# Projection, row mixing and a top-2 mixture of experts: one program section in place of two, with two expert tiles at fixed places between the last routing steps

## The chip, the cores and the metric

The program runs on one core of one Trainium2 chip. The metric is the device time of one execution in microseconds (us); less is better. Engines are named as in the profile: PE is TensorE's matrix multiply, PEld its weight load, DVE is VectorE, ACT is ScalarE, POOL is GpSimd, SP is SyncE. POOLq, SPq and so on are an engine's own queue, that is what it does beside computing: waiting, branching, issuing transfers.

## The reference, cut to what matters

```python
x = x + _L0_xattn_ref(_layernorm(x), ctx_4096, ctx_4096, Wq, Wk, Wv, Wo)   # 32 batches of 32 rows, 257 context rows, 32 heads, 8 key heads
x = x + _L0_attn_ref(_layernorm(x), eta)
x = x + _L0_ffn_ref(_layernorm(x), gate_w, expert_w)

def _L0_attn_ref(minibatch, eta):
    logits = jnp.einsum('bcl,bdl->bcd', minibatch, minibatch)
    probs = jax.nn.softmax(jnp.max(logits, axis=-1, keepdims=True) - logits, axis=-1)
    return eta * jnp.einsum('bcd,bdl->bcl', probs, minibatch) + minibatch

def _L0_ffn_ref(x, gate_w, expert_w):                     # 8 experts of 1024 x 1024, top 2
    topv, topi = jax.lax.top_k(jnp.einsum('bsh,he->bse', x, gate_w), 2)
    w_e = jnp.einsum('bske,bsk->bse', jax.nn.one_hot(topi, 8), jax.nn.softmax(topv, axis=-1))
    return jnp.einsum('bsh,eho,bse->bso', x, expert_w, w_e)
```

All is float32. x has 1024 rows (tokens) of 1024 values; each row goes to two of eight experts. With the reference's own inputs the experts get 244, 303, 297, 182, 250, 268, 260 and 244 rows; in tiles of 128 rows these are 2, 3, 3, 2, 2, 3, 3 and 2, together 20 tiles. Of the first 640 tokens, 148 go to expert 0 and 185 to expert 1.

## The kernel before, in words

The program has three sections, each a block that all engines enter and leave together: `attend` (L210), `mixing` (L874) and `experts` (L1302).

**attend** is the cross attention, up to the turned head outputs `oT`. The change touches one line of it (L525).

**mixing** works on eight tiles of 128 tokens (four batches of 32) in ten steps, t = 0 to 9, unrolled. In step t the engines handle three tiles at once, in an order written out by hand:
- PE (L1258) does the output projection of tile t in eight units of six matmuls (three passes of high and low parts, L1245), and between units the rest: before unit 2 the mixing product of tile t-2 (L1274, with the gate columns L1278), before unit 4 the transposes of the normalized rows y of tile t-1 (L1254), before unit 5 the ranking product of tile t-2 (L1266, L1267), before unit 6 the gate product (L1288, eight matmuls) and the gram product of 32 x 32 blocks (L1293) of tile t-1.
- DVE (L1103): add x to the projection and normalize it to y (L1111, L128, L132), scale and add the mixed rows (L1121), route (L1153: logits, the gap of the two best L1163, their one-hot rows), normalize to n (L132 again), low part of the next tile's oT (L1098), ranks and row numbers (L1170), the softmax shares of tile t-1 (L1135 to L1148).
- POOL (L1021): the power of -1/2 for both norms (L142), x3 = x2 + z (L1036), and two indirect DMAs per tile that put a token's number and weight into its expert's list `slot_scratch` (L1041).
- ACT (L1073): high parts, copies of transposes (L1071), exponentials, and from step 7 on the high parts of experts 0 and 1 (L1091; low parts on DVE, L871).
- SP (L981) loads x, stores n and x3 (which goes to `out_x`), and loads the raw weights of expert 0 at step 2 and of expert 1 at step 8.

After the last step PE counts the rows per expert (L1299), DVE works out a table `tiles` (L1197 to L1229: 30 small dependent instructions) that gives each tile's expert and number within the expert, and POOL gathers the rows of tile 0 (L1057).

**experts** runs 20 tiles in the order of the experts (L1474 for PE; tiles from number 8 on are behind a branch on the table). For each: gather 128 rows of n by the list into `xg` (L1369), transpose (L1469), split in high (L1408) and low (L1433), 48 matmuls of 128 x 512 (L1487), gather the rows of `out_x` into `acc` (L1387), multiply-add (L1458), and scatter them back to `out_x` (L1393). A token is in two experts, so POOL waits before each gather of `acc` for the scatter of the tile before it:

```python
            def step(i, par):                                   # POOL, L1379
                pool.wait_ge(gT_done, 2 * i + 2)
                gather(i + 2, par)
                wait_apart(pool, written, 16 * i, passed)
                ...
                pool.indirect_dma_start(acc[:, par, :], None, out, ...)
                ...
                wait_apart(pool, acc_ready, 2 * i + 2, passed)
                pool.indirect_dma_start(out, ..., acc[:, par, :], None, ...).then_inc(written, 16)
```

Weights of expert e+1 are split into the other of two slots while expert e runs: chunks 0 to 3 in its first tile's step, chunks 4 to 7 at the head of its second tile's step (L1445 to L1453 on DVE, L1418 on ACT). DVE's step i is, in this order: splits, low part of tile i+1 (L1433), splits, wait for `acc` of tile i and multiply-add.

Of the kernel before, what the change touches and what calls it, by code (L numbers as in the profile page):

```python
# [12 lines left out]
ALU = mybir.AluOpType  # L13
# [39 lines left out]
class Shared:  # L53


    def __init__(self, nc, ctx):
# [11 lines left out]
        self.tiles = sb("tiles", [1, 7, COLS], I32)  # L68

        self.first_raw = [self.at("expert0_raw", LOW0, [P, KC, D]), self.at("expert1_raw", LOW1, [P, KC, D])]  # L70
# [5 lines left out]
        self.w_h_ready, self.w_l_ready = sem("w_h_ready"), sem("w_l_ready")  # L76

        self.idx = sb("idx", [P, 2, 2], I32)
        self.xg = self.at("xg", STAGE, [P, 2, D])
        self.idx_loaded, self.xg_loaded = sem("idx_loaded"), sem("xg_loaded")  # L80


def pipelined(eng, n, step, head=1, tail=1):


    assert head % 2 == 1
    pairs = (n - head - tail) // 2
    for t in range(head):
        step(t, t % 2)
    with eng.Fori(0, pairs) as i:  # L90
        step(2 * i + head, head % 2)
        step(2 * i + head + 1, (head + 1) % 2)
    for t in range(head + 2 * pairs, n):
        step(t, t % 2)
# [12 lines left out]


class Norm:

    def __init__(self, nc, ctx, name):
        self.stats = ctx.enter_context(nc.sbuf_tensor(name + "_stats", [P, 2, 6], F32))
        self.mean_var = ctx.enter_context(nc.sbuf_tensor(name + "_mean_var", [P, 2], F32))
        self.rstd = ctx.enter_context(nc.sbuf_tensor(name + "_rstd", [P, 1], F32))
        self.var_eps = ctx.enter_context(nc.sbuf_tensor(name + "_var_eps", [P, 1], F32))
        self.minus_half = ctx.enter_context(nc.sbuf_tensor(name + "_minus_half", [P, 1], F32))
        self.eps_added = ctx.enter_context(nc.semaphore(name + "_eps_added"))
        self.passed = ctx.enter_context(nc.semaphore(name + "_passed"))  # L120
        self.stats_ready = ctx.enter_context(nc.semaphore(name + "_stats_ready"))
        self.var_ready = ctx.enter_context(nc.semaphore(name + "_var_ready"))
        self.rstd_ready = ctx.enter_context(nc.semaphore(name + "_rstd_ready"))

    def on_vector(self, dve, t, out, src):

        for h in range(2):
            dve.bn_stats(self.stats[:, h, :], src[:, h * 512:(h + 1) * 512]).then_inc(self.stats_ready, 1)  # L128
        wait_apart(dve, self.stats_ready, 2 * t + 2, self.passed)
        dve.bn_aggr(self.mean_var[:, :], self.stats[:, :, :].rearrange("p a b -> p (a b)")).then_inc(self.var_ready, 1)  # L130
        dve.wait_ge(self.rstd_ready, t + 1)
        return dve.tensor_scalar(out, src, self.mean_var[:, 0:1], self.rstd[:, 0:1], ALU.subtract, ALU.mult)  # L132

    def start_gpsimd(self, pool):
        pool.memset(self.minus_half[:, :], -0.5).then_inc(self.eps_added, 1)
        pool.wait_ge(self.eps_added, 1)

    def on_gpsimd(self, pool, t):
        wait_apart(pool, self.var_ready, t + 1, self.passed)
        pool.tensor_scalar(self.var_eps[:, :], self.mean_var[:, 1:2], EPS, None, ALU.add).then_inc(self.eps_added, 1)  # L140
        pool.wait_ge(self.eps_added, t + 2)
        pool.tensor_tensor(self.rstd[:, :], self.var_eps[:, :], self.minus_half[:, :], ALU.pow).then_inc(self.rstd_ready, 1)  # L142

class LayerNorm:

# [1385 lines left out]
```

## Time and profile before

| | us |
|---|---|
| median of 3 executions (1200.42 to 1202.53) | 1201.32 |
| the profiled execution | 1197.56 |
| its span, first to last instruction | 1195.3 |
| PE busy / DVE / ACT / POOL | 1078.9 / 683.6 / 441.2 / 265.7 |
| mean granted clock of PE, of full speed | 0.948 |

The span is what the trace shows; the profiled execution is 2.26 us longer than it. Busy shares over the whole span mix the attention section (to 717 us, not changed) with the two sections that are changed, so they say little here: the stages have to be read one by one.

### The profile page before, as it was taken

The page shows a single profiled execution, that of the slowest core. Times are in us where ns is not written, and L with a number is a line of the kernel's source. Part 1 is how long each engine was busy: PE and PEld are TensorE (multiplying, and loading weights), DVE is VectorE, ACT ScalarE, POOL GpSimd, SP SyncE. Part 2 cuts the span into 40 slices and gives each one's busy share as a digit, 9 for nine tenths or more (in the row PEclk, how much of TensorE's full clock was granted, in tenths as well). Part 3 has the DMA queues.
Part 4 walks back from the last instruction along what each step waited for, and adds up shares of the span by engine and source line. Part 5 has one row for each costly group of instructions (what it writes and reads, how often), then busy time and mean ns, then how long its engine had stood idle before and what let it go on. Part 6 is the DMA issues. An engine that isn't in the chain of part 4 may idle for free. (4 is left out here: it accounts for less than half of the span.)

```text
span 1195.3 us, 26103 instructions
## 1 busy us (share of the span) xinstructions
PE 1078.9 (90%) x9084; PEld 987.0 (83%) x9085; DVE 683.6 (57%) x1683; ACT 441.2 (37%) x1079; POOL 265.7 (22%) x454
## 2 busy tenths in 40 slices
PE   6899989999999999999999968999717988888995
PEld 5799989999999999999999947778616766766784
DVE  5541256666666666666666672787773334444441
ACT  2321245555555555555555461111240312333210
POOL 2000211111112112111111101443322333332342
PEclk9899999999999999999999968999857989999997
DMA  8233566656656755665675451653515546565422
GB/s 312 83 125 128 178 179 195 185 169 182 201 159 183 204 165 176 194 173 168 196 201 164 117 178 57 212 106 90 192 56 170 203 172 223 181 218 213 155 88 68
DMA packets 78810, 197.76 MB, mean 165 GB/s; under 512 B 14672, under 2 KB 25296, under 8 KB 74608
## 3 DMA queue, kind: packets, MB, share of 16 engines
q1 hardware_dynamic: 60688, 154.04, 41.3%
q0 software_dynamic: 18016, 42.29, 11.5%
q8 instruction: 68, 1.11, 0.4%
q14 instruction: 38, 0.31, 0.1%
HBM read 159.07 MB, written 44.56 MB: 170 GB/s over the span
## 5 line engine op out<-in xcount | busy, mean ns | idle before, releaser
L510 ACT ACTIVATE prob<-bank,nmax 128x257 f32<-128x257 f32 x256 | 122.0, 477 | 242.0 <-DVE nmax L650 241.7
L650 DVE TENSOR_REDUCE nmax<-bank 128x1 f32<-128x257 f32 x256 | 108.7, 425 | 157.2 <-PE bank L843 157.2
L1487 PE MATMUL bank<-w_h,gT_h 128*128 x320 | 132.0, 412 | 28.2 <-DVE gT_l L1433 28.2
L739 PE MATMUL bank<-wkv_h,cT_h 128*128 128x256 f32 x512 | 154.4, 302 | 0.0
L730 PE MATMUL bank<-cT_h,wkv_h 128*128 128x256 f32 x512 | 154.4, 302 | 0.0
L730 PE MATMUL bank<-cT_h,wkv_l 128*128 128x256 f32 x512 | 144.5, 282 | 0.0
L739 PE MATMUL bank<-wkv_h,cT_l 128*128 128x256 f32 x512 | 144.5, 282 | 0.0
L730 PE MATMUL bank<-cT_l,wkv_h 128*128 128x256 f32 x512 | 144.1, 282 | 0.0
L739 PE MATMUL bank<-wkv_l,cT_h 128*128 128x256 f32 x512 | 143.9, 281 | 0.0
L403 POOL DMA_DIRECT2D qcat<-q_scratch x128 | 70.4, 557 | 270.0 <-PE bank L843 267.0
L1487 PE MATMUL bank<-w_l,gT_h 128*128 x320 | 128.8, 402 | 0.0
L1487 PE MATMUL bank<-w_h,gT_l 128*128 x320 | 128.5, 401 | 0.0
L765 PE MATMUL bank<-ident,prob 128*128 128x128 f32 x512 | 101.4, 280 | 10.1 <-DVE pT L303 7.0
L1408 ACT ACTIVATE gT_h<-bank 128x512 fp32r<-128x512 f32 x42 | 22.9, 595 | 216.3 <-PE bank L1469 216.3
L1487 PEld LDWEIGHTS bank<-w_h,gT_h 128*128 128x128 f32 x320 | 62.8, 196 | 43.4 <-issue 30.9
L730 PEld LDWEIGHTS bank<-cT_l,wkv_h 128*128 128x128 f32 x512 | 97.4, 190 | 0.0
L642 DVE TENSOR_SCALAR prob<-prob,rsums 128x257 f32<-128x257 f32 x256 | 92.1, 360 | 9.1
L739 PEld LDWEIGHTS bank<-wkv_l,cT_h 128*128 128x128 f32 x512 | 97.3, 190 | 0.0
L730 PEld LDWEIGHTS bank<-cT_h,wkv_h 128*128 128x128 f32 x512 | 97.2, 190 | 0.1
L739 PEld LDWEIGHTS bank<-wkv_h,cT_h 128*128 128x128 f32 x512 | 97.2, 190 | 0.0
L730 PEld LDWEIGHTS bank<-cT_h,wkv_l 128*128 128x128 f32 x512 | 96.8, 189 | 0.0
L739 PEld LDWEIGHTS bank<-wkv_h,cT_l 128*128 128x128 f32 x512 | 96.6, 189 | 0.0
(203 smaller groups left out, 2440.6 us busy)
## 6 DMA issues: line engine op xcount, KB each, us to landing
kcat<-k_scratch SPq DMA_DIRECT2D x128, 258.0 KB, 4.2
cx<-in_context SPq DMA_DIRECT2D x32, 1024.0 KB, 7.3
raw<-in_expert_w SPq DMA_DIRECT2D x48, 512.0 KB, 6.3
qcat<-q_scratch POOLq DMA_DIRECT2D x128, 128.0 KB, 3.2
k_scratch<-kT_h SPq DMA_DIRECT2D x32, 258.0 KB, 2.8
k_scratch<-kT_l SPq DMA_DIRECT2D x32, 258.0 KB, 2.9
x_in<-in_x SPq DMA_DIRECT2D x16, 512.0 KB, 6.3
expert_raw<-in_expert_w SPq DMA_DIRECT2D x16, 512.0 KB, 8.8
```

Source lines behind the costliest of these rows:

```text
L403: pool.dma_start(qcat[c * DH:(c + 1) * DH, par, :, :].rearrange("d (g j) n -> d g (j n)", g=4).bitcast(F32), q_dram[c // 2, b].rearrange(" ...
L510: act.activation(prob[:, 1 - par, s, 0:SK], s_ps[s % 2][:, 0:SK], ACT.Exp, bias=nmax[:, 1 - par, s:s + 1], accum_out=sums[:, 1 - par, s:s ...
L642: dve.tensor_scalar(prob[:, a % 2, i, 0:SK], prob[:, a % 2, i, 0:SK], rsums[:, i:i + 1], None, ALU.mult).then_inc(prob_ready, 1)
L650: dve.reduce_max(nmax[:, 1 - par, s:s + 1], s_ps[s % 2][:, 0:SK], AXX, negate=True).then_inc(max_done, 1)
L730: o = pe.matmul(k_ps[:, j * 256:(j + 1) * 256], wkv[w][:, k, j * P:(j + 1) * P], cT[t][:, b % 2, k, :], start=(j == 0 and k == 0 and n == ...
L739: o = pe.matmul(v_ps[:, a * KV:(a + 1) * KV], cT[t][:, b % 2, k, a * P:(a + 1) * P], wkv[w][:, k, KV:2 * KV], start=(a == 0 and k == 0 and ...
L765: o = pe.transpose(turn_ps[:, c * P:(c + 1) * P], prob[:, a % 2, i, c * P:(c + 1) * P], ident[:, :])
L1408: act.activation(gT[0][:, par, h * 512:(h + 1) * 512], t_ps[h][:, :], ACT.Copy).then_inc(gT_h_ready, 1)
L1487: o = pe.matmul(y_ps[par][h][:, :], gT[a][:, par, k * P:(k + 1) * P], w[b][:, bass.ds(slot + (k * D + h * 512), 512)], start=(k == 0 and n ...
```

## The change

`mixing` and `experts` become one function `finish`, one block, with these edits:

1. **Gate columns in the gram product.** The 32 columns of each batch in `yT` get 8 gate columns beside them, so one product with 40 columns gives the gram block and the gate logits. The gate is loaded four times, once for each batch of a tile. L1288 goes.
2. **PE waits at the start.** PE waits for the constants and the small loads (gate, eta) before the projection of tile 0; before, it did so ahead of step 1.
3. **Norms.** n is made by ACT (scale and shift) in place of DVE; x3 is x2 + y on POOL, with the mixed rows added in place by DVE. The two one-hot instructions become one.
4. **Expert 0's weights early.** `oT` is laid out by tiles, its raw weights are loaded at the start, and one chunk is split in each step from 1 to 7.
5. **Two fixed tiles.** The first 128 rows of expert 0 and of expert 1 among the first five tiles of tokens are gathered in step 7 and multiplied between the last routing products. (Were there fewer than 128, the lists would be padded.)
6. **The plan** leaves these two tiles out, has 32 instructions in 11 dependent groups, and is followed by the other 18 tiles.
7. **POOL's step** gathers `acc` of tile i+1 after the scatter of tile i, and waits only for scatters of other experts' tiles, and for the buffer: `written` is one semaphore for each of the two buffers.

```diff
-        self.oT = self.at("oT", HIGH0, [P, KC, B * SQ])
+        self.oT = self.at("oT", HIGH0, [P, NT, KC, P])
...
+FIXED = 2
+EARLY = NT - 3
...
@@ SP @@
-            sp.dma_start(gate_sb[:, :, :], gate.rearrange("(c p) e -> p c e", p=P)).then_inc(small_loaded, 16)
+            for b in range(BT):
+                sp.dma_start(yT[:, :, b, SQ:GW], gate.rearrange("(c p) e -> p c e", p=P)).then_inc(small_loaded, 16)
...
+                if t == EARLY + 2:
+                    sp.wait_ge(scattered, 32 * EARLY)
+                    for i in range(FIXED):
+                        sp.dma_start(idx[:, i, :], fixed_rows(i)).then_inc(fixed_idx_loaded, 16)
+                        sp.dma_start(idx_out[:, i, :], fixed_rows(i)).then_inc(fixed_idx_loaded, 16)
...
@@ POOL @@
+            pool.wait_ge(scattered, 32 * NT)
+            pool.wait_ge(plan, PLANNED)
+            pool.wait_ge(xg_loaded, 16 * FIXED)
+            for i in range(2, 4):
+                load_idx(idx, i, i % 2).then_inc(idx_loaded, 16)
+            scatter(0, 0)
+            pool.wait_ge(gT_done, 2)
...
+            gather(2, 0)
+            pool.wait_ge(x2_ready, 2 * NT)
+            pool.wait_ge(written[0], 16)
+            gather_out(1, 1)
...
+            def step(i, par):
+                pool.wait_ge(gT_done, 2 * i + 2)
+                wait_apart(pool, xg_loaded, 16 * i + 32, passed)
+                gather(i + 2, par)
+                wait_apart(pool, written[1 - par], 8 * (i + par), passed)
+                load_idx(idx_out, i + 1, 1 - par).then_inc(idx_out_loaded, 16)
+                load_idx(idx, i + 3, 1 - par).then_inc(idx_loaded, 16)
+                other_experts = others(i + 1)
+                scatter(i, par)
+                for p in range(2):
+                    wait_apart(pool, written[p], other_experts[p], passed)
+                gather_out(i + 1, 1 - par)
...
@@ DVE, steps t = 0 to 9, then @@
+                if on(t, 1):
+                    add_x(t - 1)
+                    if t == EARLY + 2:
+                        pad_first_tiles()
+                    if t == NT:
+                        rows_low(0, 0)
+                    normalize_y(t - 1)
+                if on(t, 2):
+                    add_mixed(t - 2)
+                    route_tile(t - 2)
+                if t + 1 < NT:
+                    ot_low(t + 1)
+                if 1 <= t < NT:
+                    first_low(0, t - 1)
+                if on(t, 2) and t < NT:
+                    rank_tile(t - 2)
+                if t == NT - 1:
+                    first_low(0, NT - 1)
+                if on(t, 1):
+                    turn_shares(t - 1)
+                if t >= NT:
+                    rank_tile(t - 2)
+            add_out(0, 0)
+            rows_low(1, 1)
+            first_low(1, 0, 1)
...                                     (the plan)
+            first_low(1, 2, 3, 4, 5, 6, 7)
+            add_out(1, 1)
...
+            rows_low(2, 0)
...
@@ PE @@
-                        for k in range(KC):
-                            pe.matmul(g_ps[:, 64:64 + E], yT[:, k * P:(k + 1) * P], gate_sb[:, k, :], start=(k == 0), stop=(k == KC - 1))
+                        o = pe.matmul(g_ps[b * SQ:(b + 1) * SQ, 0:GW], yT[:, k, b, 0:SQ], yT[:, k, b, :], start=(k == 0), stop=(k == KC - 1), skip_group_check=True)
...
+            pe.wait_ge(consts, 16)
+            pe.wait_ge(small_loaded, 16 * (BT + 1))
...                                     (steps 0 to 7, units as before)
+            turn_rows(0, 0)
+            mix(NT - 2)
+            fixed_tile(0, 0, 1)
+            turn_y(NT - 1)
+            fixed_tile(0, 2)
+            products_of_rows(NT - 1)
+            fixed_tile(0, 3, 4)
+            rank(NT - 2)
+            mix(NT - 1)
+            fixed_tile(0, 5, 6)
+            rank(NT - 1)
+            fixed_tile(0, 7)
+            turn_rows(1, 1)
+            count(NT, counted)
+            fixed_tile(1, *range(KC))
+            turn_rows(2, 0)
```

In the new code `turn_rows` is the transposes of a gathered tile, `rows_low` the low part of it, `add_out` the multiply-add into `acc`, `turn_y` L1254, `mix` L1274 and L1278, `rank` L1266 and L1267, `products_of_rows` the gram product, `first_low` L871.

## Rows read from the trace of the kernel before

**Rows 1.** Windows by stage: us, busy us (instructions) per engine, PEclk, DMA share, GB/s.
```profile
720.40:748.50 28.10, 28.10 (x185) 23.31 (x186) 8.10 (x17) 2.52 (x5) 1.79 (x7) 0.90 0.15 46
748.50:850.70 102.20, 102.11 (x878) 82.31 (x877) 80.40 (x233) 17.84 (x38) 42.77 (x60) 1.00 0.48 130
850.70:906.20 55.50, 16.52 (x120) 12.20 (x118) 38.09 (x103) 16.52 (x22) 14.74 (x19) 0.54 0.37 124
906.20:1108.50 202.30, 175.78 (x785) 144.13 (x785) 88.82 (x100) 54.05 (x68) 66.96 (x71) 0.94 0.59 206
1108.50:1181.10 72.60, 72.56 (x336) 59.91 (x336) 25.88 (x33) 14.22 (x20) 27.28 (x31) 0.98 0.32 108
1181.10:1195.30 14.20, 0.00 (x0) 0.00 (x0) 0.88 (x2) 0.00 (x0) 1.02 (x1) 0.57 0.09 34
```
**Rows 2.** Waits from 906 to 1182 us: who for whom, us, times, longest.
```profile
DVE acc L1458 <- DMA acc<-out_x,idx_out: 109.9, 19, 10.1
PE bank L1487 <- DVE gT_l L1433: 28.2, 6, 6.6
```
**Rows 3.** The chain that ended last, in order of time: start, us, what.
```profile
1058.74 8.76 DMA acc<-out_x,idx_out
...
1068.50 0.75 DVE acc L1458
...
1070.18 3.41 DMA out_x<-acc,idx_out
...
1116.53 10.93 PE bank L1487 x48
1127.46 0.88 PE bank L1469 x8
```
**Rows 4.** Start of mixing: SP's and DVE's timelines, and a window.
```profile
719.31 0.70 SPq L977 DMA_DIRECT2D eta_sb<-in_eta  x1
...
724.65 1.23 DVE L1098 TENSOR_TENSOR ot_l<-oT,ot_h 128x1024 fp32r<-128x1024 f32 x1 [4.33 <-DMA eta_sb<-in_eta]
...
718.00:723.00 5.00, 2.63 (x6) 2.15 (x7) 1.22 (x1) 2.00 (x2) 2.54 (x13) 0.50 0.79 229
```
**Rows 5.** PE's timeline in step 7: start, us, line, operation.
```profile
845.26 1.85 PE L1288 MATMUL bank<-gate_sb,yT 128*128 128x8 f32 x16
847.04 0.84 PE L1293 MATMUL bank<-yT 128*32 128x32 f32 x64
847.81 0.50 PE L1245 MATMUL bank<-wo_h,ot_h 128*128 128x512 f32 x1
```
**Rows 6.** Waits of DVE for PE, steps 2 to 7 (748.5 to 850 us).
```profile
DVE x L1111 <- PE bank L1245: 1.4, 5, 0.4
DVE gated L1136 <- PE bank L1293: 1.4, 1, 1.4
```
**Rows 7.** DVE's timeline, steps 7 to 9.
```profile
840.02 1.00 DVE L1163 TENSOR_TENSOR gap<-top 128x1 f32<-128x1 f32 x1
...
844.53 0.81 DVE L132 TENSOR_SCALAR n<-x,norm_mean_var,norm_rstd 128x1024 f32<-128x1024 f32 x1 [0.98 <-POOL norm_rstd L142]
...
862.43 4.62 DVE L871 TENSOR_TENSOR w_l<-expert_raw,w_h 128x1024 fp32r<-128x1024 f32 x4
...
876.40 0.16 DVE L1163 TENSOR_TENSOR gap<-top 128x1 f32<-128x1 f32 x1
```
**Rows 8.** The plan and the first gather: DVE's and POOL's timelines.
```profile
887.41 0.17 DVE L1197 COPY counts<-bank 128x8 f32<-128x8 f32 x1 [0.75 <-PE bank L1299]
...
894.36 0.17 DVE L1229 CAST tiles<-only 1x26 int32<-1x26 f32 x1
...
897.11 1.07 POOL L1057 DMA_INDIRECT xg<-n_scratch,idx  x1 [2.33 <-DMA idx<-slot_scratch]
```
**Rows 9.** DVE's timeline at a change of expert.
```profile
952.76 1.41 DVE L1458 SCALAR_TENSOR_TENSOR acc<-bank,idx_out,acc 128x512 f32<-128x512 f32 x2 [7.42 <-DMA acc<-out_x,idx_out]
955.94 4.63 DVE L1439 TENSOR_TENSOR w_l<-raw,w_h 128x1024 f32 x4 [1.77 <-issue]
```

More of the change, by code:

```diff
@@ L863 @@
 COLS = MT + AHEAD
-ROWS = (E - 1) * B * SQ + (COLS - E + 1) * P
-def split_low(dve, sh, e, c):
-    high, low = (part[:, e * SLOT + c * D:e * SLOT + (c + 1) * D] for part in sh.w)
-    dve.wait_ge(sh.w_h_ready, KC * e + c + 1)
-    dve.tensor_tensor(low, sh.first_raw[e][:, c, :], high.bitcast(F32), ALU.subtract).then_inc(sh.w_l_ready, 1)
-def mixing(nc, sh, x, eta, gate, expert_w, out, n_dram, slot_dram):
+ROWS = (E - 1) * B * SQ + (COLS - E + 2) * P
+FIXED = 2
+EARLY = NT - 3
+NEVER = 1e6
+GW = SQ + E
@@ L953, in mixing @@
[L953 to L962 removed]
+        small_loaded, slots_cleared, consts = sem("small_loaded"), sem("slots_cleared"), sem("consts")
+        ot_h_ready, ot_l_ready, xo_done = sem("ot_h_ready"), sem("ot_l_ready"), sem("xo_done")
@@ new lines, in finish, with entry, planned_tiles, step_if_used @@
+        written = [sem("written0"), sem("written1")]
+        PLANNED = 32
+        def on(t, lag):
+            return 0 <= t - lag < NT
+        def entry(eng, i, what, most):
+            return eng.value_load(tiles[0:1, what, bass.ds(i - FIXED, 1)], min_val=0, max_val=most)
+        def planned_tiles(eng, step):
+            def step_if_used(i, par):
+                if known(i) and i < FIXED + E - 1:
+                    step(i, par)
+                else:
+                    with eng.If(entry(eng, i, 3, 1) > 0):
+                        step(i, par)
+            eng.wait_ge(plan, PLANNED)
+            last = FIXED + MT
+            step_if_used(2, 0)
+            with eng.Fori(0, (last - 3) // 2) as pair:
+                step_if_used(2 * pair + 3, 1)
+                step_if_used(2 * pair + 4, 0)
+            for i in range(3 + (last - 3) // 2 * 2, last):
+                step_if_used(i, i % 2)
@@ L1000, in _ @@
+            with sp.Fori(3, E) as e:
+                for c in range(KC):
+                    sp.wait_ge(w_l_ready, KC * e - KC + c + 1)
+                    load_chunk(e, c)
         @block.gpsimd
@@ new lines, in _ @@
+            then(dve.tensor_tensor(start[:, :, :], reached[:, :, :], begin_b, ALU.mult),
+                 dve.tensor_reduce(expert[:, :], reached[:, :, :], AXX, ALU.add))
+            then(dve.tensor_reduce(opened[:, :], start[:, :, :], AXX, ALU.max),
+                 dve.tensor_scalar(tiles[:, 0, :], expert[:, :], -1.0, None, ALU.add),
+                 dve.tensor_scalar(splits[:, :], expert[:, :], float(E), None, ALU.is_lt),
+                 dve.tensor_tensor(only[:, 0:COLS - 1], expert[:, 1:COLS], expert[:, 0:COLS - 1], ALU.is_gt))
@@ new lines, in rank, with count @@
+            def rank(t):
+                pe.wait_ge(both_ready, t + 1)
+                pe.matmul(e_ps[:, rank_cols], earlier[:, :], both[:, :], start=True, stop=False)
+                pe.matmul(e_ps[:, rank_cols], ones[:, :], before[:, :], start=False, stop=True).then_inc(rank_done, 1)
+            def count(tiles_ranked, signal):
+                pe.wait_ge(rows_ready, tiles_ranked)
+                pe.matmul(e_ps[:, count_cols], ones[:, :], before[:, :], start=True, stop=True).then_inc(signal, 1)
@@ new lines, in _ @@
+            pe.wait_ge(consts, 16)
+            pe.wait_ge(small_loaded, 16 * (BT + 1))
+            for t in range(NT):
+                for unit in range(KC):
+                    if unit == 1 and t == EARLY + 2:
+                        count(EARLY, early_counted)
+                    if unit == 2 and on(t, 2):
+                        mix(t - 2)
+                    if unit == 4 and on(t, 1):
+                        turn_y(t - 1)
+                    if unit == 5 and on(t, 2):
+                        rank(t - 2)
+                    if unit == 6 and on(t, 1):
+                        products_of_rows(t - 1)
+                    product(t, unit)
@@ L1504, in program @@
         attend(nc, sh, x, wq, wk, wv, wo, context, q_dram, k_dram, vlast_dram)
-        mixing(nc, sh, x, eta, gate, expert_w, out, n_dram, slot_dram)
-        experts(nc, sh, expert_w, n_dram, slot_dram, out)
+        finish(nc, sh, x, eta, gate, expert_w, out, n_dram, slot_dram)
 def kernel(**inputs):
```

911 lines of the change are left out of this document (461 added, 450 removed).

## The prediction, made before the changed kernel was run

> **What bounds the kernel now.** Differences are taken against the profiled execution (1197.56 us, span 1195.3); the median of the three runs is 3.8 us above it, and the forecast is given for the median. A measurement of this kernel can tell about 0.2% (2.4 us) from no change.
>
> I read the stages first [rows 1]. In steps 2 to 7 of mixing (748.5 to 850.7) PE is busy all the time at full clock: 102.2 us, or 17.03 a step. From the end of the last projection (850.7) to the first expert matmul (906.2) it is busy 16.5 of 55.5 us at about half clock: a chain of routing, planning and gathering, with nothing to fill PE. Then come 20 expert tiles in two regimes. A tile costs PE 10.93 us of matmuls and 0.88 of transposes [rows 3], 11.81. The last six take 72.6 us, 12.1 each: PE's pace. The first fourteen take 202.3, or 14.45 each, which is 37 us too much.
>
> Why is in the waits [rows 2]. DVE waits 109.9 us for `acc`, and PE in turn 28.2 us, in six pieces, for low parts that DVE makes late. The chain shows what paces DVE [rows 3]: gather `acc` (8.8), multiply-add (0.75, second half), scatter (3.4), the next gather, because each gather waits for the scatter of the tile before. With some 1.7 us between the links this is 14.6 us a tile. At a change of expert DVE, released late at 952.8, still has four splits and the next low part to do [rows 9], and PE runs dry. The 37 us are these 28.2 and about 9 of matmuls at the lower clock after each stall.
>
> **The change, part by part.**
>
> *Start, +7.4.* Before, nothing on PE waited for the small loads until step 1; DVE saw the last one (eta) land at 724.65 [rows 4]. Now PE's first product waits for it, and three more gate loads stand before it in SP's queue. The DMA engines work 0.79 of the 5 us from 718 to 723, 4.0 us [rows 4]; two x tiles of 512 KB at some 400 GB/s are 2.6 of these, so one gate load with eta and the cleared lists is at most 1.4, and I take 1.05 for each gate load: 3.1 more, landing near 727.8. PE started at 720.4 [rows 1]. Bounds: +4.3 if the loads overlap wholly, +12 if each costs the 1.4 and up to 0.7 of issue (as eta's) on top. All later work hangs on this, so it counts in full. Raw weights of expert 0 now follow in the queue, behind what is waited for.
>
> *Steps 1 to 7, -10.* The gate product takes 1.78 us a step (845.26 to 847.04), the gram product 0.77 [rows 5]. With 40 columns for 32 the latter is at most a quarter longer, 0.96. That frees 1.6 us of PE a step. DVE lies just beneath: it waited for PE only 2.8 us in six steps [rows 6], so it needs 16.6 of the 17.03. It loses n (0.73 from start to start) and the wait for POOL before it (0.98) [rows 7], and one of two one-hot instructions (0.25), and gains a chunk's split (1.15 each in the four at 862.4 [rows 7]): 15.8. PE would need 15.4. One more thing: the gap of the two best takes 1.00 us at 840.02 and 0.16 at 876.40 [rows 7]; in the first case POOL was adding x3 at the time. POOL now adds right after y, beside instructions that read PSUM, and is done before routing: up to 0.8 less, and DVE at 15.0 is no longer the bound. So PE's 1.6 times 7 is 11.2, less about 1 for the padding instructions, one early count and small waits: 10. Bounds: 8 (DVE decides) and 12. The Trainium skill (SBUF — State Buffer, "The single rule" and its consequences) says that a DVE instruction with two SBUF inputs is blocked by a GpSimd instruction that reads SBUF, and one with a single SBUF input is not. By that rule, the trace agrees (1.00 against 0.16), and the contention goes; without it the steps would give 8 and not 10. The ranking product before unit 5 wants both one-hot rows; they come after the statistics of x3 now, 1.3 us later than before, against a slack of about as much. Fixed gathers: POOL waits in step 7 for the lists of five tiles, but has nothing due until the statistics of tile 7.
>
> *From the last projection to the first tile after the plan, 55.5 to 53: -2.5.* PE: transposes of fixed tile 0 when its rows are there (+2), mixing 6 (2), chunks 0 and 1 (a chunk is 10.93/8 = 1.37), turn y (1), chunk 2, gram (1), chunks 3 and 4, rank, mixing 7: about +19 with a few us at the lower clock. DVE then needs 1.4 + 1.5 + 3 for the add, statistics and routing of tile 7: rank at +25, chunk 7, transposes of fixed tile 1 and the count: +29. DVE: add into `acc` (1.4), low part (1.3), two splits (2.3): +33. The plan took 7.15 us (887.41 to 894.56) [rows 8]; with 32 instructions in 11 dependent groups, 0.2 for each group and 0.1 for each that follows within one, and 0.2 more for the wide ones, I take 5.2: +38. Meanwhile PE stands after chunk 1 of fixed tile 1, for six splits are queued behind the plan on DVE. Then six chunks at 1.37 (the splits, 1.15, keep ahead) and 3 us of lower clock: +50. Beside it POOL: two list loads, 2.3 us of waiting (as before the gather at 897.11 [rows 8]), scatter 0, gather of tile 2, then `acc` of fixed tile 1, on which DVE waits ahead of tile 2's low part: +51 to +56. I take 53; bounds 46 and 64.
>
> *Two tiles fewer after the plan, -23.6* (2 x 11.81): their matmuls lie in that gap.
>
> *Pace of the rest, -32.7.* Before, 274.9 us for 20 tiles [rows 1], 38.7 above 20 x 11.81. Now a gather of `acc` waits for a scatter only where the expert changes. Within an expert, from the end of a tile's matmuls: add 1.4, 0.6, issue of the scatter 1.3, gather 8.8: 12.1, due at 11.8 + 1.4 with nothing behind it. At a change: 1.4 + 0.6 + 3.4 + 0.5 + 8.8 = 14.7, so 2.9 late; then DVE adds (1.4), turns to the splits (1.8), makes four (4.6) and the low part (1.3) [rows 9], done at 12.0 after PE's end of that tile, against 11.8. So it just fits even with the slow gather, and lateness no longer adds up from tile to tile. I leave 1.9 for the first tile's clock (the excess of the last six, 72.6 - 6 x 11.81 = 1.7, shows what one restart costs) and 4 for small stalls: 6. Bounds 2 and 28. Bytes: 1.5 MB a tile and 4 MB an expert; 18 tiles are 51 MB, 240 GB/s at PE's pace, against 206 now at 0.59 DMA share [rows 1]: 0.69.
>
> *End, 0*: the last scatter and 14.2 us after PE's end [rows 1] stay.
>
> Sum: 7.4 - 10 - 2.5 - 23.6 - 32.7 = -61.4. The profiled execution would be 1136.2, the median **1140**.
>
> **Rivals.**
> - *Half the stalls stay.* The gather after a change shares the DMA engines with a 2 MB burst of raw weights; if it takes 3 us more, PE stalls 3 us at each of the six or seven changes, with 1.5 of lower clock each (9 us over six stalls before): about 26, not 6. Time 1160. For: 8.8 us gathers beside weight loads; against: slack of the three-tile experts.
> - *The fixed tiles don't run in the gap*: lists or rows of x3 land late, PE stands at the first transposes, in order, and the tail is about 24 longer: 1164. For: four list loads sit on SP behind a wait for the scatters of tile 4; against: these are issued some 16 us before PE needs them.
> - *Better than summed*: small loads overlap, few stalls, tail 47: 1125.
> - *Slower.* One queue carries the gather of `xg`, the scatter and the gather of `acc`. If these now run one behind another, as `acc` is asked for only after the scatter is issued, a tile takes 8.8 + 3.4 + 8.8 = 20.9 us [rows 3]: 901.1 + 18 x 20.9 + 14.2, span 1291, median 1298. It decides from a tile period of 15.6 us ((1195.3 - 14.2 - 901.1)/18). Against: the same three already pass in 14.45 a tile, and in 12.1 over the last six [rows 1].
>
> **How the numbers follow.** Forecast 0.60 (its own range 1128 to 1152), half the stalls 0.20, fixed tiles late 0.06, better 0.08, slower 0.03, and 0.03 for mishaps that eat the gain but no more. The range from 1124 to 1167 leaves out a part of the better case, the slower one and the worst of the middle ones. Faster by over 0.2%: 0.95; within 0.2%: 0.02; slower: 0.03.
>
> **What would show it.** Start: PE's first projection near 728, released by eta's landing. Steps: 15.5 us from one mixing product to the next, no line for the gate. Tail: projection matmuls and expert matmuls mixed, an idle stretch of PE under the plan, the plan in 5 us. Rest: 18 tiles in some 219 us, waits of DVE for `acc` well under 109.9 us and no scatter-gather pairs in the chain save at changes of expert. It is wrong if DVE, not PE, has no idle time in steps 2 to 7, if a tile still takes over 13 us, or if the tail is over 64.

## The result and the profile after

The changed kernel takes 1165.04 us (median of 4 runs, 1162.25 to 1168.08) against 1200.87 for the kernel before beside it: ratio 0.9705, 95% interval 0.9674 to 0.9736. It is faster by 35.8 us; 61.4 were forecast. The profiled execution took 1164.72 us, its span is 1163.2, 32.1 less than before.

The stages, as in [rows 1], with the steps of mixing one by one (window: its length, then busy us and instructions of each engine, PE's granted clock, DMA share, GB/s):

```profile
721.40:729.70 8.30, 0.00 (x0) 0.03 (x1) 1.22 (x1) 1.12 (x2) 2.53 (x16) 0.65 0.76 162
729.70:758.40 28.70, 28.70 (x181) 23.26 (x182) 12.31 (x22) 6.47 (x9) 6.38 (x7) 0.92 0.45 171
758.40:776.20 17.80, 15.34 (x131) 11.75 (x130) 12.34 (x38) 4.66 (x8) 7.59 (x11) 1.00 0.26 81
776.20:795.80 19.60, 17.11 (x132) 12.99 (x132) 13.24 (x39) 4.66 (x8) 8.70 (x13) 0.91 0.46 90
...
867.90:919.05 51.15, 35.96 (x215) 26.97 (x214) 34.76 (x107) 15.25 (x22) 18.47 (x25) 0.89 0.82 257
919.05:1144.60 225.55, 217.45 (x1008) 180.24 (x1008) 103.17 (x119) 66.20 (x84) 86.46 (x90) 0.98 0.53 187
1144.60:1163.20 18.60, 0.00 (x0) 0.00 (x0) 0.75 (x1) 0.00 (x0) 2.10 (x2) 0.57 0.07 26
```

The windows give the sum. x's load for mixing is issued at 721.42, 3.4 us later than before, although the code up to there is the same; over the twelve executions profiled below it lies between 717.97 and 722.07, so this is scatter between executions. Start (load to first projection) 8.28 against 2.39: +5.9. First projection to the end of the last 138.2 against 130.3: +7.9, where -10 was forecast. Tail 51.15 against 55.5: -4.3. Rest 225.55 for 18 tiles against 274.9 for 20: -49.4. End 18.6 against 14.2: +4.4. Together -32.1.

A step has one mixing product, so their distance is the period: 17.9 and 19.5 us in turn, 18.6 on average, where 17.03 stood before and 15.5 was forecast. PE's own work in a step is 15.34 us at full clock (15.4 was forecast); the rest is idle time, and in every second step a stretch at the lower clock (0.91 granted, 17.11 busy). The waits from 729 to 868 us say where it is lost (who for whom, us in total, times, longest):

```profile
DVE gated L1341 <- remote: 15.8, 5, 3.2
PE bank L1483 <- DVE x L1266: 12.4, 5, 2.5
```

And this is one step in order of time (start, us, engine, line, operation, idle time before it and who ended it):

```profile
767.24 0.80 PE L1505 MATMUL bank<-yT 128*32 128x40 f32 x64
767.97 1.14 POOL L1054 DMA_INDIRECT slot_scratch<-entries,slot  x1 [4.08 <-DVEq L1336]
769.41 0.97 POOL L1054 DMA_INDIRECT slot_scratch<-entries,slot  x1 [0.30 <-issue]
770.71 0.17 DVE L1341 COPY gated<-bank 128x8 f32<-128x8 f32 x1 [3.10 <-remote]
773.45 0.47 PE L1483 MATMUL bank<-wo_h,rows_h 128*128 128x512 f32 x1 [2.46 <-DVE x L1266]
```

The gram product is over at 768.04. DVE's copy of the gate columns waits for its signal and for nothing else that is late, and starts at 770.71; the profile, which finds no instruction that ended just then, writes "remote". In the 2.6 us between, DVE stands. The trace's semaphore events show that it is the signal that is late, and not DVE: the increment for the product comes at 770.69, 2.65 us after the product's end (2.65 to 2.68 in steps 2 to 6), and the copy 0.02 us behind it. All of DVE's work of the step moves back, x2 (x plus the projection, L1266) too, and PE stands 2.46 us for x2 in the next step. In step 1 the copy starts at once (752.79 after a product from 751.95 to 752.75). Beside steps 2 to 6 there lies what step 1 has not: GpSimd's two slot scatters. No line of the kernel makes the one wait for the other. In steps 7 and 8 other indirect DMAs of GpSimd lie beside the product (gathers for the fixed tiles, then the scatters; in step 8 the gather of `acc`), and there PE itself stands between the small products:

```profile
860.41 0.84 PE L1505 MATMUL bank<-yT 128*32 128x40 f32 x48
861.04 1.15 POOL L1054 DMA_INDIRECT slot_scratch<-entries,slot  x1 [0.30 <-issue]
861.70 0.30 PE L1505 MATMUL bank<-yT 128*32 128x40 f32 x6 [0.44 <-issue]
...
876.62 0.94 PE L1505 MATMUL bank<-yT 128*32 128x40 f32 x50
878.00 0.38 PE L1505 MATMUL bank<-yT 128*32 128x40 f32 x14 [0.44 <-issue]
```

### The profile page after: what moved, and what is told of

Its sections match the earlier page's. It is cut to its first block and busy times, and to the rows that moved or that the text cites. A ratio compares the mean times of both kernels' runs of the same rounds, so it can differ in the third digit from the quotient of the medians.

```text
span 1163.2 us, 26007 instructions
## 1 busy us (share of the span) xinstructions
PE 1064.0 (91%) x8958; PEld 971.0 (83%) x8959; DVE 665.3 (57%) x1671; ACT 449.1 (39%) x1087; POOL 270.3 (23%) x454
## 3 DMA queue, kind: packets, MB, share of 16 engines
q8 instruction: 66, 1.08, 0.4%
## 5 line engine op out<-in xcount | busy, mean ns | idle before, releaser
L1604 PE MATMUL bank<-w_h,rows_h 128*128 x288 | 115.3, 400 | 3.8 <-DVE rows_l L1373 3.8
L1604 PE MATMUL bank<-w_h,rows_l 128*128 x288 | 113.3, 393 | 0.0
L1604 PE MATMUL bank<-w_l,rows_h 128*128 x288 | 113.3, 393 | 0.0
L1209 ACT ACTIVATE rows_h<-bank 128x512 fp32r<-128x512 f32 x42 | 23.1, 596 | 180.2 <-PE bank L1539 169.2
L522 DVE TENSOR_TENSOR cT_l<-bank,cT_h 128x512 fp32r<-128x512 f32 x128 | 87.0, 681 | 9.4 <-ACT cT_h L404 9.4
```

The source lines that it names most:

```text
L522: dve.tensor_tensor(cT[1][:, b % 2, 2 * m:2 * m + 2, :].rearrange("p a n -> p (a n)"), cT_ps[m % 2][:, :], high, ALU.subtract).then_inc(cT ...
L1209: act.activation(gT[0][:, par, h * 512:(h + 1) * 512], t_ps[h][:, :], ACT.Copy).then_inc(gT_h_ready, 1)
L1604: o = pe.matmul(y_ps[par][h][:, :], gT[a][:, par, k * P:(k + 1) * P], w[b][:, bass.ds(slot_at + (k * D + h * 512), 512)], start=(k == 0 an ...
```

## Experiments

Ratios are to the kernel before, run on the same chip; where a row tells more than the ratio, it stands there. Most ratios are known to 0.003, or 3 us, two only to 0.007, and differences of ratios and of medians differ by some 3 us too: the gain of experiment 1 over the changed kernel is 19 us by the ratios and 15.9 by the medians.

**1. Scatters after the signal.**

```
+                    pool.wait_ge(g_done, min(t, NT))
                     scatter_slots(t - 2)
```

> The open point is why the signal of the gram product reaches DVE 2.6 us after its last matmul in steps 2 to 6 (steps 1 and 8 show no delay, and no slot scatter lies beside them). Here GpSimd issues its two slot scatters of a step only once that signal has arrived. Theory A (GpSimd's indirect DMAs, 768.0 to 770.4 beside a product that ends at 768.0, hold the signal back): DVE copies `gated` within 0.2 us of the product's end, PE's 2.5 us wait for x2 goes, the period of a step falls from 18.6 to between 15.5 and 16, the time falls by 14 to 19 us. Theory B (the delay is PE's own: the signal comes with the twelfth projection matmul behind the gram product, whatever GpSimd does): the wait of 3.1 us stays, the scatters move 2.7 us later, the time moves by less than 3 us.

Measured: 1149.11 us, ratio 0.9546 (0.9519 to 0.9573), 0.0159 or 19 us below the changed kernel. The timelines of PE, DVE and GpSimd in step 3, and steps 2 to 6 as a window:

```profile
782.35 0.80 PE L1506 MATMUL bank<-yT 128*32 128x40 f32 x64
783.20 0.17 DVE L1342 COPY gated<-bank 128x8 f32<-128x8 f32 x1 [0.51 <-PE bank L1506]
783.53 1.09 POOL L1054 DMA_INDIRECT slot_scratch<-entries,slot  x1 [4.56 <-PE bank L1506]
...
758.20:834.86 76.66, 76.66 (x654) 59.18 (x652) 62.27 (x192) 23.79 (x40) 36.41 (x51) 1.00 0.47 100
```

A wait was added and the kernel became faster. The signal is prompt, PE has no idle time over five steps (76.66 of 76.66), the period is 15.29 us (15.33 over the five). Theory B falls. From the first projection to the last it is 118.7 us and not 138.2; of these 19.5 us the tail (57.6) gives back 6.4 and the rest (228.5) 3.0. (The profiled execution took 1153.8 us, the slowest of the six, so its stages show less gain than the median.)

**2. Gram product ahead of the scatters.**

```
-                    if unit == 6 and on(t, 1):
+                    if unit == 5 and on(t, 1):
                         products_of_rows(t - 1)
```

> The gram product goes behind the ranking product of unit 5 instead of unit 6, 1.4 us earlier, so that eighteen projection matmuls follow it in the step, and it is over before GpSimd is told to scatter the slots. Theory A (GpSimd's scatters hold the signal): no delay any more, DVE finds the signal set when it comes to it, period 15.5 to 16, time 14 to 19 us less. Theory B (tied to PE's own order, as 3.5 us after the product's start): the signal comes near 769.3 instead of 770.7, DVE still waits some 1.7 us, PE's wait shrinks from 2.5 to about 1.1, time 6 to 9 us less; if it is tied to the last matmul of the step, nothing changes.

Measured: 1149.4 us, 0.9554 (0.9525 to 0.9582). The period is 15.03 us; in steps 2 to 6 DVE finds the signal set, so here too theory B falls. In step 7 the product now lies beside the gathers for the fixed tiles, with the slot scatters right behind them (843.33 to 845.79), and there the hold stays:

```profile
841.21 0.91 PE L1505 MATMUL bank<-yT 128*32 128x40 f32 x63
842.59 0.21 PE L1505 MATMUL bank<-yT 128*32 128x40 f32 x1 [0.47 <-issue]
846.28 0.17 DVE L1341 COPY gated<-bank 128x8 f32<-128x8 f32 x1 [2.70 <-remote]
```

Keeping the two apart in time is enough, whichever is moved. A gather can hold too: the last product stands 0.47 us for nothing else (the gathers are issued from 840.38 to 843.03). The signal then comes 0.47 us after the end of the second scatter.

**3. Gate product apart again**, gram of 32 columns, one gate load.

```
+                for k in range(KC):
+                    pe.matmul(g_ps[:, SQ:GW], yT[:, k, :, :]..., gate_sb[:, k, :], ...)
-                        o = pe.matmul(g_ps[..., 0:GW], yT[:, k, b, 0:SQ], yT[:, k, b, :], ...)
+                        o = pe.matmul(g_ps[..., 0:SQ], yT[:, k, b, 0:SQ], yT[:, k, b, :], ...)
```

> The gate product is a product of its own again (8 products of 128 x 8), ahead of a gram product of 32 columns with its rows packed as before; one gate load instead of four, waited for at the same place. Start: PE begins 3.2 us earlier (three issues of 1.08 us less on SP's queue). Theory C (the wider rows of 40 columns bring the late signal): PE does 1.7 us more a step, the signal is prompt, period 17.0, so the steps are 1.6 us a step shorter than in the changed kernel and the time falls by 3 + 11 = 14 us. Theories A and B: the delay of 2.6 us stays, as DVE still comes to its wait during the gram product or the scatters lie beside it; period 18.6 to 20, time between 3 us less and 7 us more.

Measured: 1170.33 us, 0.9738 (0.9709 to 0.9767); period 18.9. Theory C falls: a product of 32 columns is caught too. It comes later in the step, in the middle of the scatters, and here the trace shows the hold on PE itself in every step from 2 to 7:

```profile
783.06 1.09 POOL L1055 DMA_INDIRECT slot_scratch<-entries,slot  x1 [3.99 <-DVEq L1337]
784.07 0.58 PE L1508 MATMUL bank<-yT 128*32 128x32 f32 x42
784.46 0.96 POOL L1055 DMA_INDIRECT slot_scratch<-entries,slot  x1 [0.30 <-issue]
785.09 0.28 PE L1508 MATMUL bank<-yT 128*32 128x32 f32 x6 [0.44 <-issue]
785.82 0.36 PE L1508 MATMUL bank<-yT 128*32 128x32 f32 x16 [0.45 <-issue]
```

64 small products that take 0.76 us alone take 2.1: after 42 of them PE stands, does six, stands, and does the rest once the second scatter is over. "issue" says that PE waited for nothing that the profile knows. The start missed its forecast: with one gate load in place of four the first projection comes 7.36 us after x's load and not 8.28, so 0.9 us earlier where 3.2 were expected.

**4. Only the second scatter later**, to see how long the hold is.

```
                 for c in range(2):
+                    if c == 1:
+                        pool.wait_ge(g_done, min(t + 2, NT))
```

> The changed kernel, with the second slot scatter of each step issued only when the gram product's signal has come; the first stays where it is (768.0 to 769.1). Both runs that kept the scatters off the end of the gram product had a prompt signal, so the scatters hold it. What is open is how long. Theory A1 (the signal is held for as long as GpSimd works on indirect DMAs, and some 0.4 us more): it now comes 0.4 us after the first scatter's end, 1.4 us after the product instead of 2.6; DVE waits 1.9 us, not 3.1, PE 1.2, not 2.5, the period falls from 18.6 to between 16.5 and 17.3, the time by 7 to 11 us. Theory A2 (once a scatter has caught the signal it comes with the twelfth matmul behind the product): the signal stays at 3.47 us after the product's start, the time moves by less than 3 us.

Measured: 1157.18 us, 0.9634 (0.9608 to 0.9660), 8.5 us below the changed kernel; period 16.6.

```profile
782.77 0.80 PE L1507 MATMUL bank<-yT 128*32 128x40 f32 x64
783.45 1.09 POOL L1056 DMA_INDIRECT slot_scratch<-entries,slot  x1 [4.06 <-DVEq L1338]
784.89 0.17 DVE L1343 COPY gated<-bank 128x8 f32<-128x8 f32 x1 [1.78 <-PE bank L1507]
```

The product ended at 783.57, the scatter at 784.54, and the copy starts 0.35 us after that. With both scatters it started 0.33 to 0.51 us after the second's end. The last rows of a scatter land some microseconds later still (10.5 us after the last one's issue in the changed kernel), so it is GpSimd's instruction and not the transfer that the signal follows. The delay follows the scatters' end, as A1 had it; A2 falls.

**5. The kernel before, with its gate and gram products one unit later** (`unit == 7` for `unit == 6`).

> The kernel before, with its gate and gram products moved behind unit 6, 1.4 us later, so that the gram product ends while the first slot scatter of the step is issued; in the kernel before, the scatter began 0.3 us after the signal in steps 2 to 6 (gram product ended at +0.76, signal at +0.78, scatter from +1.0 to +1.2). In its step 7 the scatter ran from 0.13 us before the product to 0.15 us after it and the signal was prompt. Theory A1 (a signal that falls due beside a scatter comes some 0.3 us after the scatter's end): the signal comes 0.4 us or more late in steps 2 to 6, or the product itself breaks into pieces. Theory H (only the changed kernel's product is caught): every signal is prompt, as in that step 7.

Measured: 1222.82 us in one run, 21 above the median of the kernel before beside it; mixing products 20.8 us apart and not 17.03.

```profile
766.77 1.14 POOL L1041 DMA_INDIRECT slot_scratch<-entries,slot  x1 [3.57 <-DVEq L1185]
767.13 0.60 PE L1293 MATMUL bank<-yT 128*32 128x32 f32 x44
768.05 0.26 PE L1293 MATMUL bank<-yT 128*32 128x32 f32 x4 [0.32 <-issue]
768.21 0.96 POOL L1041 DMA_INDIRECT slot_scratch<-entries,slot  x1 [0.30 <-issue]
768.76 0.28 PE L1293 MATMUL bank<-yT 128*32 128x32 f32 x5 [0.45 <-issue]
769.50 0.43 PE L1293 MATMUL bank<-yT 128*32 128x32 f32 x11 [0.46 <-issue]
769.97 0.17 DVE L1136 COPY gated<-bank 128x8 f32<-128x8 f32 x1 [3.55 <-PE bank L1293]
```

So the hold has nothing to do with the changed code. The kernel before escaped it by 0.2 to 0.5 us: in steps 2 to 6 its scatters began that long after the product's end, right behind DVE's copy (762.95, the product having ended at 762.51). The change made the step shorter on DVE, so that the slots are ready sooner, and dropped the gate product in front of the gram: in steps 2 to 6 the first scatter now begins 0.07 to 0.16 us before the product's end, and the two met.

**6 and 7. Start.** First the small loads alone are waited for at first use (on PE, ScalarE and DVE); then, on top of experiment 1, GpSimd's constants too (the first line below goes in the second kernel alone; PE's waits move to `mix(0)` and `products_of_rows(0)`).

```
-            pe.wait_ge(consts, 16)
-            pe.wait_ge(small_loaded, 16 * (BT + 1))
```

> PE, ScalarE and DVE wait for the small loads (gate columns four times, eta) only at their first use, in step 1, and not ahead of the first projection. The first projection then starts 2.4 us after x's loads are issued and not 8.3 us. Theory: the whole of the 5.9 us is on the path, the time falls by 5.5 to 6.5 us. Rival: the raw weights of expert 0 or the small rows of 32 bytes that are still landing slow something else (ot or x2), and less than 3 us come back.

Measured: 1162.35 us, 0.9674 (0.9645 to 0.9703), 3.7 us less, with intervals that overlap. Before PE's first projection, 2.66 us after the load, now stands

```profile
723.89 0.80 PE L1485 MATMUL bank<-wo_h,rows_h 128*128 128x512 f32 x1 [3.39 <-POOL steps L1016]
```

which is a wait that lay hidden behind the first. Long as it looks, it costs 0.27 us: without it the first projection comes 2.39 us after the load, since PE would stand 3.12 us there for the low parts of tile 0 (next run). 5.6 us are gained at the start, and 0.6, 1.1 and 0.8 are lost again in the steps, the tail and the rest.

> Scatters after the gram signal, and small loads and constants waited for at their first use on PE, ScalarE and DVE. Where only the small loads had been moved, PE stood 3.4 us for the last constant that GpSimd writes, and 3.7 us came back (0.9674 against 0.9705). Theory: with the constants' wait moved too, the first projection starts 2.4 us after x's load as in the kernel before, and the time is 5.5 to 6.5 us below that of the kernel with the later scatters alone (ratio near 0.950 against 0.9546). Rival: the steps take no profit, as the raw weights of expert 0 or something later sets the time of the tail: under 3 us.

Measured: 1144.86 us, 0.9547 (0.9510 to 0.9584), against 1149.11 and 0.9546 without it. The first projection starts 2.39 us after the load, as expected, and the span fell by 9.2 (1143.0), but the ratios show no gain, and the medians 4.3 us: whether all of the 5.9 us comes back stays open by these runs. (Of the 9.2, some 5.9 lie at the start and 3.3 in the 18 tiles, which the edit does not touch.)

**8 and 9. Raw weights of expert 2 behind the small transfers of the tail**, on top of 1 (first try, below) and of 1 and 7 (second, with `xg_loaded, 16 * (FIXED + 1)` in place of `scattered, 32 * NT`).

```
             sp.wait_ge(x3_ready, 2 * NT)
+            sp.wait_ge(scattered, 32 * NT)
             for c in range(4):
                 load_chunk(2, c)
```

In the changed kernel GpSimd stands 11.74 us, for the slots' landing above all, and 4.4 beyond the end of the plan (898.9), before it loads the first list; then rows and low parts are late (GpSimd's and PE's timelines):

```profile
890.60 0.95 POOL L1054 DMA_INDIRECT slot_scratch<-entries,slot  x1 [0.30 <-issue]
903.29 0.60 POOL L1063 DMA_DIRECT2D idx<-slot_scratch  x1 [11.74 <-issue]
...
914.12 1.10 PE L1539 MATMUL bank<-ident,xg 128*128 128x128 f32 x8 [3.90 <-DMA xg<-n_scratch,idx]
919.05 0.79 PE L1604 MATMUL bank<-w_h,rows_h 128*128 x1 [3.84 <-DVE rows_l L1373]
```

> Scatters after the gram signal, and the raw weights of expert 2 are asked for only when the last slot scatter has landed. In the changed kernel that landing took 10.5 us (14.4 with the later scatters), and GpSimd waited for it until after the plan, so the lists, the gather of tile 2 and its first matmul come late. Theory D (the 2 to 4 MB of raw weights in flight hold the small scattered rows back): the landing takes 6 us or less, the plan ends GpSimd's wait (near 881 in place of 888.5), tile 2's first matmul comes 5 to 8 us earlier, the time falls by 5 to 8 us. Theory E (the landing is slow by itself, from its 256 small descriptors, or from expert 1's weights): the lists come at the same time, the time changes by less than 2 us, or grows if expert 2's splits become late.

Measured: 1150.82 us, 0.9571 (0.9542 to 0.9601), no gain over 0.9546. GpSimd's timeline:

```profile
872.91 0.96 POOL L1055 DMA_INDIRECT slot_scratch<-entries,slot  x1 [0.30 <-issue]
882.91 0.60 POOL L1064 DMA_DIRECT2D idx<-slot_scratch  x1 [9.05 <-issue]
...
892.26 1.06 POOL L1076 DMA_INDIRECT xg<-n_scratch,idx  x1 [4.89 <-DMA idx<-slot_scratch]
```

The list is asked for 9.0 us after the end of the last scatter in place of 14.4, and the last rows of that scatter land 6.2 us after its issue in place of 13.2, so D is right on the landing. But now the burst begins just then and falls on the lists: the tail is 58.2 us for 57.6. D and E's prices both hold, D's for the transfer and E's for the time.

> Scatters after the gram signal, loads and constants waited for at first use, and the raw weights of expert 2 asked for only when the rows of tile 2 have landed (not, as in the run before, when the slots have, where the burst fell on the lists and on that gather). Theory D2 (in the tail every small transfer beside the burst is late, so the burst has to stay behind the first gather too): slots land 5 us after their issue, tile 2's rows before PE has done with fixed tile 1, tile 2's first matmul comes some 50 us after the last projection in place of 57, the time falls by 5 to 8 us against the same kernel without this edit (1144.9, profile span 1143.0). Rival: it is paid back at the first change to expert 2, whose weights then come late (a stall of over 5 us at the sixth or seventh tile), or the gather of `acc` for fixed tile 1, behind the others in GpSimd's queue, sets the end: under 3 us.

Measured: 1137.92 us, 0.9458 (0.9388 to 0.9527); that is 6.9 us under 1144.86, with intervals that overlap. The gather of tile 2 is issued at 884.92, 14.8 us after the last scatter, against 19.4 in the first try; the tail takes 53.8 us against 56.9. It is not the 50 expected: now the rows of fixed tile 0 are late for faster steps, and PE stands 5.53 us for them at 846.59. The rest is 1.5 us longer (226.8 for 225.3), with no stall of over 5 us more at a change of expert.

**10 and 11. Rows of tile i + 3 asked for ahead of the scatter of tile i**, on top of 1; the second time on top of 1 and 7, with the list a step earlier too.

```
-                gather(i + 2, par)
...
+                pool.wait_ge(gT_done, 2 * i + 4)
+                wait_apart(pool, xg_loaded, 16 * i + 48, passed)
+                gather(i + 3, 1 - par)
                 scatter(i, par)
```

> Scatters after the gram signal, and GpSimd asks for the rows of tile i + 3 ahead of the scatter of tile i, so never behind the wait for the scatters of the expert before. Theory F (of the 13 us that the 18 tiles take above 18 x 11.81, the stalls at 967 and 1056 of 4.6 and 5.2 us come from that order in GpSimd's queue: 4 us of waiting, then a gather of 8 us): they go, 18 tiles take 215 to 218 us instead of 225.6, the time falls by 7 to 10 us. Rival G (the gathers beside a burst of raw weights are late whatever the order, or the accumulator rows become what is late): stalls of 3 us or more stay at the expert changes, and less than 4 us come back.

Measured: 1203.98 us, 1.0012 (0.9989 to 1.0034). All of the gain is gone, and 18 tiles take 271.9 us. Theory F is not tested by this: the list of the rows is now asked for just ahead of them, which is a wait of its own (the second line). The waits of that stretch:

```profile
DVE acc L1386 <- DMA acc<-out_x,idx_out: 117.7, 16, 13.0
POOL xg L1075 <- DMA idx<-slot_scratch: 45.1, 17, 5.3
```

> Scatters after the gram signal, loads and constants at first use, and again the gather of rows one step earlier, ahead of the scatter; this time its list is loaded a step earlier too (the first try made GpSimd wait 45 us in 17 pieces for lists just asked for). Theory F (the stalls at the expert changes come from the gather of rows standing behind the wait for the scatters): 18 tiles in 215 to 219 us against 225.3, time 6 to 9 us less. Theory G2 (the scatter and the gather of `acc` now stand behind 0.5 MB of rows in the same queue, and they are what paces a tile): DVE's waits for `acc` grow beyond 60 us, 18 tiles take over 230 us, the time rises by 5 us or more.

Measured: 1148.27 us, 0.9574 (0.9505 to 0.9642), 3.4 us above 1144.86, with intervals that overlap; 18 tiles in 229.7 for 225.3. The tile periods at the changes of expert are 16.4 and 16.3 us, as before the edit (16.9 and 16.1), and the tile behind each now takes 13.5 and 14.5 where it took 11.8. F falls: the order in GpSimd's queue does not cause these stalls. DVE's waits for `acc` came to 43.0 us (38.8 without the edit) and not to over 60, so G2's size was off and its sign right. The rows beside a burst of raw weights take 8.2 us (in the changed kernel, shown below); that this is the whole cause was not isolated.

**12. All that helped**, and the gram product of steps 1 to 6 ahead of unit 5.

> All that helped, together: slot scatters only after the gram signal, small loads and constants waited for at first use, the raw weights of expert 2 behind the rows of tile 2, and the gram product behind the ranking product of unit 5 in steps 1 to 6 (in step 7 it stays ahead of unit 6, since there the gathers of the fixed tiles would lie beside it). Theory: first projection 2.4 us after x's load, mixing products 15.0 us apart (15.29 with the later scatters alone), first matmul of tile 2 some 54 us after the last projection, 18 tiles in 225 to 228 us, end 18.6 us. The time is 1 to 2 us under that of the kernel without the moved gram product (1137.9), ratio to the kernel before 0.943 to 0.948. Rival: the rows of fixed tile 0 land no sooner, so what the steps save PE waits at the first transposes: no difference from 1137.9.

Measured: 1136.02 us (1135.6 to 1138.27, 6 runs), 0.9440 (0.9408 to 0.9472): 66.7 us below the kernel before, 0.0265 or 32 us below the change as it stood (29 by the medians). By stages, from the first projection to PE's end (before them lie 2.39 us of start, behind them 18.60 of end):

```profile
722.37:750.45 28.08, 28.08 (x180) 22.95 (x181) 12.25 (x22) 5.49 (x8) 6.44 (x10) 0.94 0.62 206
750.45:825.93 75.48, 75.48 (x653) 60.34 (x652) 61.80 (x192) 23.80 (x40) 36.49 (x51) 1.00 0.49 103
825.93:838.77 12.84, 12.84 (x119) 9.55 (x117) 10.70 (x34) 2.77 (x6) 9.22 (x11) 1.00 0.41 133
838.77:888.33 49.56, 36.21 (x215) 27.39 (x215) 34.88 (x107) 15.21 (x22) 19.31 (x26) 0.92 0.63 195
888.33:1115.70 227.37, 218.97 (x1008) 180.94 (x1008) 103.16 (x119) 66.08 (x84) 85.69 (x90) 0.97 0.57 202
```

Steps, rest and end came as expected, and the tail shorter (49.6 for 54): the rows of fixed tile 0 are there 2.4 us after the last projection and not 5.5. The difference to experiment 9 is within the intervals.

## Why the prediction was right in sign and range, and its gain 1.7 times the measured one

- **Start**, +7.4 forecast, +5.9 measured. Right in what PE waits for: eta, the last in SP's queue (issued at 726.64), releases the first projection. The term that was mis-sized is the 3.1 us for three more gate loads. They do cost 1.08 us each in issue (four in 4.33), but their landings overlap: eta lands 3.0 us after its issue, where it took 5.3 before and 6.0 in experiment 3. From x's load to eta's landing it is 8.2 us with four gate loads, 6.6 in the kernel before and 7.3 in experiment 3 with one, so three of them cost 0.9 to 1.6.
- **Steps**, -10 forecast, +7.9 measured: here the prediction failed, and by 17.9 us this is more than the other misses together. Its reckoning of work was right: 15.3 us of PE a step, DVE beneath it, and, as forecast from the contention for SBUF, the gap of the two best at 0.16 us in all eight tiles (159 to 161 ns, where POOL's add beside it had made it 1.00). The step that failed is "PE's 1.6 times 7 is 11.2, less about 1 for ... small waits". It took a signal to be there when its product ends. I moved GpSimd's scatters and the gram product against each other on paper (the slots ready sooner, the gate product gone) and never asked what lies beside the gram product now. [Rows 5] were read for durations only. Experiments 1, 2 and 4 show the cause, experiment 5 shows it in the kernel before, and with the scatters moved the same stretch takes 118.7 us against 130.3 before: -11.6, within the bounds of 8 and 12.
- **Tail**, 53 forecast, 51.2 measured, within 46 to 64, but set by something else than the forecast's end. The plan took 4.8 us (5.2 forecast, from 894.1 to 898.8), and PE stood 2.73 us just before it and 2.73 us across its end, both times for low parts of weights. What ended the tail was the chain slots, list, rows; "two list loads, 2.3 us of waiting" left out that the slots of the last tile must land first, beside raw weights at a DMA share of 0.82.
- **Two tiles fewer**, -23.6: they ran in the gap, from 871.40 and 893.18. Held.
- **Pace of the rest**, 6 us above 18 x 11.81 forecast, 13 measured, within 2 to 28. A gather of `acc` no longer paces a tile: DVE's waits for it fell from 109.9 [rows 2] to 31.1 us. The term was mis-sized by a wait that had no line in the sum: at two changes of expert the rows `xg` came late. The chain there, in order of time:

```profile
948.06 6.91 DMA out_x<-acc,idx_out
...
961.20 3.23 DMA out_x<-acc,idx_out
...
967.69 8.23 DMA xg<-n_scratch,idx
...
976.05 1.54 PE bank L1539 x8
```

  These two tiles took 16.4 and 17.0 us, two more 13.3 and 13.6, all others 11.8.
- **End**, 0 forecast, +4.4 measured. The gather of `acc` for a tile that does not exist is now asked for behind the last scatter (1147.75 after 1146.40), which by its issue would be 1.35 us of it; no run takes it away, and the other 3 were not looked into.
- **Rivals.** "The fixed tiles don't run in the gap" gave 1164, nearest by number and by chance alone: they did run there. "Half the stalls stay" gave 1160, but only 7 of its 20 us came. The slower one (a tile of 20.9 us) did not come: the three transfers pass side by side. None of the rivals named the hold. So that 1165.04 lies in the range of 1124 to 1167, 2 us from its end, is in part luck: the room above the forecast was left for other causes.
- The test named for the steps ("if DVE, not PE, has no idle time in steps 2 to 7") did not catch it either: both had idle time.

## What to carry to other kernels

Where a step is re-timed, list for every engine what now runs beside each short product, GpSimd's indirect DMAs above all, and read the wait behind it in the new trace before anything else is tuned. A wait whose releaser the profile cannot name, and that stops with the end of another engine's instruction, is worth one run that moves that instruction. A wait that is taken away shows the next one, and a burst of weights moved off one small transfer falls on the next, so such edits are measured one on another.

## What the runs showed of the hardware

- While GpSimd issues indirect DMAs (scatter or gather, about 1 us each), PE's run of 64 small products can be held up (41 to 50 pass, mostly, then a few at a time with 0.4 us of standing between), or it is over and its signal comes only 0.3 to 0.6 us behind the end of the last indirect DMA, some 2.65 us late with two and 1.3 with one. The projection products behind it go on at their pace meanwhile (a start every 0.23 us from 768.30 to 770.60). The Trainium skill (SBUF — State Buffer, "SBUF: two separate sides") says that PE never waits on anyone for SBUF; by that the hold would have another seat than the SBUF ports. No run here shows its seat.
- Not every meeting has an effect. In step 7 of the kernel before, the gram product (847.04) lies wholly beside a scatter (from 846.91) and DVE's copy starts at once, at 847.92; in step 7 of experiment 1 a product of 0.80 us lies beside a gather (843.49 to 845.46) and has a prompt signal too, and so have the products of 0.82 to 1.12 us beside a gather in step 7 of experiments 7 to 12. Being beside an indirect DMA is needed in all fourteen traces (no product without one is broken up or has its signal over 0.04 us late), but not always enough; what decides stays open.
- GpSimd's arithmetic did not hold it: in step 1 of experiments 2 and 12 the whole product lies beside the add for x3 (in experiment 2 from 1.3 us before the product to 0.2 after it), takes 0.80 us and has a prompt signal.
- Where PE stands 2.5 us in each step, the granted clock is lower in every second step (0.91 and 1.00 in turn, so a part of it at 1.2 GHz in place of 2.4), which cost some 1.7 us of busy time each (17.11 for 15.34); steps without idle time hold 1.00.
